# A graph layer on one core: the edge-attribute bias moved from VectorE to GpSimd, and small VectorE operations given a second source tile

## What is computed

```python
h = jnp.maximum(_layernorm(x, axis=-1), 0.0)
# the layer on h
xn = layernorm(h, g1, b1)
msg = jax.nn.relu(xn[src] + edge_attr)
aggr = jax.ops.segment_sum(msg, dst, num_segments=N)
y = (1.0 + eps_gin) * xn + aggr
y = jax.nn.relu(y @ Wg1 + bg1) @ Wg2 + bg2
h = h + y
xn2 = layernorm(h, g2, b2)
f = jax.nn.gelu(xn2 @ Wf1 + bf1, approximate=False) @ Wf2 + bf2
out = x + h + f
```

## Time and profile before

| what | value |
|---|---|
| three runs | 1066.06, 1067.87, 1068.01 us; median 1067.87 us |
| the profiled execution | 1065.76 us, its span 1064.0 us, so 1.76 us lie around the span |
| busy share of the span | PE 93%, PEld 80%, DVE 92%, ACT 79%, POOL 75% |
| mean granted TensorE clock | 0.979 |

### The profile page before, as it was taken

The page is one execution under the profiler, slowest core; times in us unless marked ns, Lnnn a source line. Parts: engine busy times, 40 slices in busy tenths (PEclk is TensorE's granted clock), DMA queues, the critical chain, the costliest instruction groups (busy, mean ns, idle before and its releaser), DMA issues. The chain is left out here.

```text
span 1064.0 us, 23086 instructions
## 1 busy us (share of the span) xinstructions
PE 992.4 (93%) x6684; PEld 852.4 (80%) x6684; DVE 978.6 (92%) x3499; ACT 844.1 (79%) x2158; POOL 800.9 (75%) x510
## 2 busy tenths in 40 slices
PE   1456999999999999999999999999999999999998
PEld 0345888888888888888888888888888888888887
DVE  5679999999999999999999999999999999998752
ACT  1247888888888888888888888888888888878773
POOL 6588878878878778878878878878878878876610
PEclk9758999999999999999999999999999999999999
DMA  7565667778887555554554564654654654443311
GB/s 262 165 182 136 185 177 182 211 223 236 250 229 196 142 140 114 146 140 114 146 140 113 147 140 113 146 140 113 147 139 112 146 140 114 115 109 92 59 57 40
DMA packets 110468, 156.87 MB, mean 147 GB/s; under 512 B 24835, under 2 KB 50607, under 8 KB 110334
## 3 DMA queue, kind: packets, MB, share of 16 engines
q1 hardware_dynamic: 70358, 128.99, 37.4%
q0 software_dynamic: 37760, 25.66, 19.4%
q10 hardware_dynamic: 2216, 0.66, 0.3%
HBM read 90.61 MB, written 64.61 MB: 146 GB/s over the span
## 5 line engine op out<-in xcount | busy, mean ns | idle before, releaser
L521 ACT ACTIVATE n_act<-p_f,bf1e_col 128x512 f32<-128x512 f32 x392 | 255.9, 679 | 149.6 <-PE p_f L882 144.8
L926 PE MATMUL p_out<-wf,n_act 128*128 128x128 f32 x3136 | 370.5, 276 | 0.0
L446 POOL DMA_INDIRECT aggr_sums<-e_merged,e_index x196 | 323.7, 1652 | 59.7 <-issue 49.9
L926 PEld LDWEIGHTS p_out<-wf,n_act 128*128 128x128 f32 x3136 | 357.7, 191 | 3.9
L455 POOL TENSOR_TENSOR n_rstd<-n_var,minus_half 128x12 f32<-128x12 f32 (+2 forms) x102 | 256.6, 2515 | 114.5 <-DVE n_var L829 57.8
L435 POOL DMA_INDIRECT e_x<-in_x,e_cols x196 | 214.7, 1095 | 60.1 <-issue 59.1
L882 PE MATMUL p_f<-n_z2T_high,wf_low 128*128 128x512 f32 x392 | 207.5, 529 | 10.7 <-issue 6.7
L882 PE MATMUL p_f<-n_z2T_high,wf_high 128*128 128x512 f32 x392 | 155.2, 396 | 0.0
L882 PE MATMUL p_f<-n_z2T_low,wf_high 128*128 128x512 f32 x392 | 154.4, 394 | 0.0
L674 DVE BATCH_NORM_STATS2 n_stat<-n_x 128x6 f32<-128x256 f32 x392 | 139.6, 415 | 0.1
L571 ACT ACTIVATE n_relu<-n_x,n_minus 128x128 f32<-128x128 f32 x392 | 124.7, 396 | 12.5 <-DVE n_minus L812 12.5
(11 more groups left out here) (85 smaller groups left out, 1432.5 us busy)
## 6 DMA issues: line engine op xcount, KB each, us to landing
n_x<-in_x SPq DMA_DIRECT2D x97, 256.0 KB
n_aggr<-aggr_sums SPq DMA_DIRECT2D x97, 256.0 KB
out_dram<-n_out SPq DMA_DIRECT2D x97, 256.0 KB
aggr_sums<-zeros SPq DMA_DIRECT2D x26, 512.0 KB, 5.8
e_dst<-in_dst_rows SPq DMA_DIRECT2D x49, 256.0 KB
e_attr<-in_attr SPq DMA_DIRECT2D x48, 256.0 KB
aggr_sums<-zeros SPq DMA_DIRECT2D x12, 1024.0 KB
e_x<-in_x,e_cols POOLq DMA_INDIRECT x196
```

The costliest lines, as they stand in the source:

```text
L446: nc.gpsimd.indirect_dma_start(out=aggr, out_offset=bass.IndirectOffsetOnAxis(ap=e_index[0:r, s, j:j + 1], axis=0), in_=e_merged[0:r, s, j ...
L521: nc.scalar.activation(n_act[:, k, :, 0:b.rows], p_f[k % 2][:, :, 0:b.rows], ACT.Gelu, bias=bf1e_col[:, k:k + 1]).then_inc(s_act, 1)
L926: last = nc.tensor.matmul(p_out[0:b.rows, j, :], n_act[:, k, j, 0:b.rows], wf2[:, k, :], start=False, stop=(k == KF - 1), skip_group_check ...
```

## The change

One tile addition per chunk (49 in all) goes from VectorE's stream to GpSimd's. In GpSimd's even step it stands behind the two gathers, and in the starting steps, where both halves are in one step, ahead of the scatters and of the second two gathers. Its waits are the same three: the row b1, the attributes, and e_sum of the chunk three earlier. Seven small VectorE operations on 128x4 keep their results and change their form: each had one source tile and immediate values, and now reads a constant from a second tile. Three constant tiles are filled at the start.

```diff
+        minus_one, eps_tile, eps_eps_tile = (sb(n, [P, J]) for n in ("minus_one", "eps_tile", "eps_eps_tile"))
...
@@ GpSimd, step
                 if 0 in halves and (c := edge(0)) is not None:
                     gather(c, range(0, PAIR))
+                if 0 in halves and (c := edge(2)) is not None:
+                    r, s = c.rows, c.slot(3)
+                    if c.is_number(0):
+                        pool.wait_ge(s_rows_out, 1)
+                    pool.wait_ge(q_attr[s], 16 * (c.uses(3) + 1))
+                    reached(pool, s_esum, c.at - 2)
+                    nc.gpsimd.tensor_tensor(e_attrb[0:r, s], e_attr[0:r, s], all_columns(b1_row, r),
+                                            ALU.add).then_inc(s_eattrb, 1)
                 if 1 in halves and 0 in halves:
                     merged_first(edge, apart)
@@ VectorE
+            for tile, value in ((minus_one, -1.0), (eps_tile, EPS), (eps_eps_tile, EPS * EPS)):
+                nc.vector.memset(tile[:], value).then_inc(s_tiles, 1)
...
             dve.wait_ge(s_const, 8)
+            dve.wait_ge(s_tiles, 3)
...
-                    nc.vector.tensor_scalar(n_var[0:r, s, 0], n_stat[0:r, s, 0, :, 2], 1.0 / D, EPS,
-                                            ALU.mult, ALU.add).then_inc(s_nvar0, 1)
+                    nc.vector.scalar_tensor_tensor(n_var[0:r, s, 0], n_stat[0:r, s, 0, :, 2], 1.0 / D, eps_tile[0:r],
+                                                   ALU.mult, ALU.add).then_inc(s_nvar0, 1)
...
-                    nc.vector.tensor_copy(e_dstf[0:r, s], e_cols[0:r, s, 1, :]).then_inc(s_ecopy, 1)
-                    nc.vector.tensor_scalar(e_minus[0:r, s], e_stat[0:r, s, 0, :, 1], -1.0, None,
+                    nc.vector.tensor_tensor(e_dstf[0:r, s], e_cols[0:r, s, 1, :], minus_one[0:r],
+                                            ALU.max).then_inc(s_ecopy, 1)
+                    nc.vector.tensor_tensor(e_minus[0:r, s], e_stat[0:r, s, 0, :, 1], minus_one[0:r],
                                             ALU.mult).then_inc(s_eminus, 1)
...
-            def add_b1(c):
...
-                    nc.vector.tensor_tensor(e_attrb[0:r, s], e_attr[0:r, s], all_columns(b1_row, r),
-                                            ALU.add).then_inc(s_eattrb, 1)
...
                     first_half(edge(1), node)
-                    if 0 in halves:
-                        add_b1(edge(2))
```

More of the change, by code:

```diff
@@ L213, in gnn_kernel @@
         p_f = [pb(f"p_f{i}") for i in range(2)]
-        (s_row_param, s_node_param, s_row_one, s_spread, s_rows_out, s_const, s_ones, s_eps, s_scaled_params, s_b1g, s_b2f, s_wf1, s_wf1_mean, s_bf1, s_bias, s_zeros, s_seeded,
+        (s_row_param, s_node_param, s_row_one, s_tiles, s_spread, s_rows_out, s_const, s_ones, s_eps, s_scaled_params, s_b1g, s_b2f, s_wf1, s_wf1_mean, s_bf1, s_bias, s_zeros, s_seeded,
          s_order_in, s_bounds, s_order, s_bad, s_flag) = (sem(f"s_{n}") for n in (
-             "row_param", "node_param", "row_one", "spread", "rows_out", "const", "ones", "eps", "scaled_params", "b1g", "b2f", "wf1", "wf1_mean", "bf1", "bias", "zeros", "seeded",
+             "row_param", "node_param", "row_one", "tiles", "spread", "rows_out", "const", "ones", "eps", "scaled_params", "b1g", "b2f", "wf1", "wf1_mean", "bf1", "bias", "zeros", "seeded",
              "order_in", "bounds", "order", "bad", "flag"))
@@ L713, in first_half @@
                     dve.wait_ge(s_estat, c.at + 1)
-                    nc.vector.tensor_copy(e_dstf[0:r, s], e_cols[0:r, s, 1, :]).then_inc(s_ecopy, 1)
-                    nc.vector.tensor_scalar(e_minus[0:r, s], e_stat[0:r, s, 0, :, 1], -1.0, None,
+                    nc.vector.tensor_tensor(e_dstf[0:r, s], e_cols[0:r, s, 1, :], minus_one[0:r],
+                                            ALU.max).then_inc(s_ecopy, 1)
+                    nc.vector.tensor_tensor(e_minus[0:r, s], e_stat[0:r, s, 0, :, 1], minus_one[0:r],
                                             ALU.mult).then_inc(s_eminus, 1)
-                    nc.vector.tensor_scalar(e_var[0:r, s, 0], e_stat[0:r, s, 0, :, 2], EPS / D, EPS * EPS,
-                                            ALU.mult, ALU.add).then_inc(s_evar0, 1)
+                    nc.vector.scalar_tensor_tensor(e_var[0:r, s, 0], e_stat[0:r, s, 0, :, 2], EPS / D, eps_eps_tile[0:r],
+                                                   ALU.mult, ALU.add).then_inc(s_evar0, 1)
                 z2_low(node)
@@ L811, in step @@
                     dve.wait_ge(s_nstat, b.at + 1)
-                    nc.vector.tensor_scalar(n_minus[0:r, s], n_stat[0:r, s, 0, :, 1], -1.0, None,
+                    nc.vector.tensor_tensor(n_minus[0:r, s], n_stat[0:r, s, 0, :, 1], minus_one[0:r],
                                             ALU.mult).then_inc(s_nminus, 1)
@@ L828, in step @@
                     dve.wait_ge(s_stat2, b.at + 1)
-                    nc.vector.tensor_scalar(n_var[0:r, after_three(b), 2], n_stat2[0:r, b.slot(8), :, 2], 1.0 / D, EPS,
-                                            ALU.mult, ALU.add).then_inc(s_var2, 1)
+                    nc.vector.scalar_tensor_tensor(n_var[0:r, after_three(b), 2], n_stat2[0:r, b.slot(8), :, 2], 1.0 / D,
+                                                   eps_tile[0:r], ALU.mult, ALU.add).then_inc(s_var2, 1)
                 if (b := node(7)) is not None:
```

## The result

The changed kernel takes 1120.8 us (median of four runs, 1119.11 to 1121.83) against 1067.91 us before: a ratio of 1.0498, with a 95% interval from 1.048 to 1.0516. It is 5% slower, and the range on record ended at 1083. Its profiled execution has a span of 1119.4 us, 55.4 more than before.

The account below looks back on a forecast made before the run. VectorE was taken to set the pace, TensorE right behind and GpSimd next. Terms of -4.5, +3.1 and +0.7 us gave -0.7 us: 1065.1 us for the profiled execution, 1067.2 us on the median, range 1062 to 1083.

Parts of the forecast that it names:

- The rival in which the two engines get in each other's way at SBUF: Odd step: VectorE stands still during GpSimd's addition, 0.7 to 1.3 us a pair; 1079 us, chance 0.20.
- 19.18 + 0.24 + standstill: VectorE's pair: its need without the addition, present gaps and the standstill; 20.1 to 20.7 us.
- a small reader on GpSimd delays nobody: Evidence against SBUF interference: L842 took 0.70 us beside a power of 12 columns, as elsewhere.
- The small operations: Seven VectorE operations given a second source: gain between nothing and 0.1 us a pair, taken as 0.
- the second source moves them from the free to the wrong side: Small VectorE operations with two SBUF inputs would now contend with a GpSimd instruction that reads SBUF; no separate size.
- The addition's length: GpSimd's 128x512 addition: 1.3 us taken, with 0.74 to 2.3 us kept for the rivals.
- The case of a long addition: Rival: an addition over 1.6 us makes GpSimd set the pace; at 1.9 us, 1082 us; chance 0.13.
- 18.29 + 1.3 = 19.6 us: GpSimd's pair in the even stretch: own work plus the addition, below TensorE's 19.91 us, so hidden.
- Gain: Even stretch: VectorE loses the addition, TensorE's 19.91 us a pair limits the gain to 0.11 us; -4.5 us over 41 pairs.
- the ramp: Start of the even stretch: additions in GpSimd's full stream delay gathers that VectorE waits for; +3.1 us.
- the last chunk: End of the even stretch: the addition stands ahead of GpSimd's power at 928.75 and the gathers behind it; +0.7 us.
- SyncE's queue: Load of e_attr and those behind it move by up to 4.3 us: 0; without a step's cover, up to 4 us a pair.

Follow-up runs that it names:

- the good one: Changed kernel with the addition moved to GpSimd's even step, behind the power of 16 columns: ratio 0.9924 to the kernel before; 0.993 with one-source small operations.
- the memset: Against the changed kernel, the addition stays on VectorE and GpSimd fills an unread 128x1400 scratch tile with zeros at its place: 1072.8 us, ratio 1.0043.

## Why the prediction was wrong

**The mechanism was on the list, and its price and chance were too small.** The rival in which the two engines get in each other's way at SBUF had a chance of 0.20, a standstill of 0.7 to 1.3 us and 1079 us. Its own formula, 19.18 + 0.24 + standstill, gives 21.09 us a pair with the measured 1.67. The standstill lies above its upper end, because VectorE stopped ahead of the addition's reported start; from the reported start alone it would be 1.25 us, inside the rival's range.

**The step that failed** is the evidence against that rival: L842 kept its 0.70 us beside a power, "so a small reader on GpSimd delays nobody", and the unlengthened L842 then spoke against a block by the addition as well. Two things were wrong with it. First the order: in the earlier trace rows L842 starts at 928.50 and the power at 928.75, so by the rule that the prediction itself names it was the power that had to wait. It did, with 2.62 us instead of 2.31, as the powers with such a start do in the other kernels. That row spoke for the block, and could not speak against it. Second the kind of instruction: in the earlier trace rows L842 did come second, but 0.56 us behind the start of the power, and a power lets VectorE pass 0.2 us behind its start. It has 12 or 16 columns to read; the addition has 512 of each source, and the same operation of the same two tiles took 1.50 us beside it. The length of a GpSimd instruction on the timeline doesn't tell how long it uses what VectorE needs.

**The small operations.** 0 was right: ratios of 1.0006 alone, 1.0526 against 1.0498 with the addition at the place of the change, 0.993 against 0.9924 at the good one. The thought beside it, that the second source moves them from the free to the wrong side, fell: with one source n_var stood 1.82 us too, so it had not been on the free side before (the last point of this text has what the Trainium skill says of such forms).

**The addition's length.** 1.3 us was taken, 1.26 to 1.29 measured. The case of a long addition is out, and so is GpSimd as the limit at this place: 18.29 + 1.3 = 19.6 us against a pair of 21.09. The limit itself is real, and was summed too low: where the load was moved, GpSimd needs 20.31 us a pair without a pause. Of the 0.7 us above 19.6, the power that grew from 2.31 to 2.69 us is 0.4: it is the wait behind the residual sum, which the sum of GpSimd's work had at nothing. The rest is in longer DMA instructions: the gathers ahead of the two powers are shown with 1.14 and 1.25 us instead of 1.04, and a scatter with 1.70 instead of 1.58; why was not looked into.

**Gain.** The sum had -4.5 us from a floor of 19.91 us a pair. The floor is lower: the kernel with the addition behind the even power has 19.89 in the mean over 42 pairs and 19.83 in most, and from it the pairs gained 840.6 - 835.2 = 5.4 us. So the gain was there to be had, and somewhat larger than forecast; at the place of the change it was buried under the standing.

**Ramp and last chunk.** +3.1 us were forecast for the ramp; with the memset, which takes GpSimd's time and stops nobody, the first p_out comes at 101.8 instead of 98.7, +3.1. (VectorE keeps its own additions in that kernel, for which the forecast had taken off 0.6.) That the forecast fits to the tenth is partly luck: with the addition behind the even power the first p_out comes at 96.4 to 99.8 in three kernels that do the same work in the middle. The changed kernel has +7.1. In its ramp, too, VectorE stands beside four of the five additions for 1.7 to 1.8 us and beside the fifth for 0.7; that this makes the other 4 us is likely, but no run shows it alone. For the last chunk +0.7 stood against +3.4 measured; but this pair takes 23.3 us (+1.6) even in the kernel that changes the small operations alone, and +2.0 with the memset, so at least part is the order in which the last gathers meet the powers, and the term was not a price of the addition only.

**SyncE's queue.** 0 with a cover of one step held at the place of the change. The price named if the cover fails, "up to 4 us a pair", was paid by the kernel with the addition behind the odd power, and most of the 40 us that moving the load gave back is 0.9 us in each of 42 pairs (21.08 - 20.17).

## What to carry to other kernels

Before work is moved from VectorE to GpSimd, list what VectorE runs in those microseconds: the move costs the standing of whatever cannot pass (here 0.5 to 2.3 us for an instruction of 1.3 to 1.8), and gains only if that is less than what leaves VectorE. Put the GpSimd instruction beside statistics or PSUM evacuations, and look in the profile for a tiny operation with a mean several times its usual one: a full VectorE may be a standing one. Before two overlapping instructions are read as proof that they don't disturb each other, look which started first: only the second could have been stopped, and it may be the GpSimd one. That a power or another short reader has delayed nobody says nothing of an instruction that streams a large tile. And whoever waits for the moved result (here SyncE's load) has to be followed to the new place.

## What the runs showed of the hardware

- A 128x512 addition on GpSimd, mostly 1.26 to 1.29 us, stops a VectorE operation of four columns with one source or with two, the match matrices and the two-tile L846 until 0.1 to 0.2 us before its reported end: 1.67 us in the changed kernel, 2.34 ahead of the gathers (where the addition is shown with 1.83), 0.98, 0.80 and 0.5 elsewhere. The statistics keep 0.75 us and n_out 0.68 beside it. A write-only instruction of 1.28 us does not lengthen n_var, n_out or the residual sum.
- Behind a gather or a scatter the standing begins before the addition's reported start: at least 0.42 us before in the changed kernel (n_var shown from 620.18, usually done in 0.07, the addition from 620.67), at least 0.41 ahead of the gathers (607.26 + 0.27 against 607.94). Where the addition had to wait for n_var, this early standing was gone (0.16 us instead of 1.82 at the same distance from the gather's end and from the addition). The Trainium skill has an explanation, Perfetto Trace Analysis, GPSIMD Engine Instruction and DMA Instruction — SWDGE (GPSIMD): GpSimd is eight processors with a queue each and no synchronization between them, two of which prepare the descriptors of a DMA, and the reported start is that of the first. By it the other six can begin to read while the gather is still shown. No run here separates the processors, so this stays an inference; and in no run with a power ahead of the addition did VectorE have an operation there that could have shown an early stop.
- The block works both ways, and it is the second one that waits. A power of 12 columns, 2.31 us alone, becomes 2.85, 2.70, 2.62 and 2.49 us when it starts 0.02, 0.16, 0.25 and 0.37 us behind the two-tile residual sum, which keeps its 0.70. A power that starts first costs the residual sum 0.03 to 0.04 us at a distance of 0.05, and nothing from 0.19 on: it blocks for its first tenth or two of a microsecond, and not until its end. The rule as the prediction quotes it has the later one blocked throughout; for a power that comes first the rows don't bear that out.
- Why the one-source small operations are stopped and the statistics are not is shown by no run. The Trainium skill, SBUF — State Buffer, Who interferes with whom, says that casts and one-source arithmetic can use the ports shared with GpSimd in some of their modes, and the rows agree with that for both: 0.68 us for the cast beside the addition, 1.82 for the arithmetic.
